# Idle products, an earlier root and earlier sums in the drain of a fused tower kernel, a second PSUM bank for two image pieces, and a last tile in halves

## The chip, the cores and the metric

One Trainium2 chip, one of its cores. The metric is the device time of one execution in microseconds (us), the median of several runs; lower is better.

## The reference

A batch of 64 images of 2 x 104 x 104 goes through three layers (fp32). `tok`: each image is stacked with its four shifts, normalised over all of it, scaled and shifted by maps, and cut into 8 x 8 patches by a convolution, which gives 169 tokens of 128. `attn`: attention with exponential features, 8 heads of 64. `ffn`: a mixture of 8 experts, 2 for each token.

```python
h = tok(x)                                         # [64, 169, 128]
n = layernorm(h)
q', k' = exp(q @ projT), exp(k @ projT)            # q, k, v from n @ WqkvT, by head
out = (q' @ (k'T @ v)) / (q' @ sum(k') + 1e-6)
h = h + out @ WoutT + bout
n = layernorm(h)
topv, topi = top_k(n @ Wg, 2); w = softmax(topv)
for e in experts:
    y += gw[..., e] * ((silu(n @ W[e]) * (n @ V[e])) @ W2[e])
h = h + y
```

## The kernel before, in words

**Tokens.** Two images (338 tokens) are a pair; there are 32 pairs, in 8 groups of 4. Each engine runs a program of its own, and semaphores order them. A loop of steps `n = 0 .. 34` is a software pipeline: in step `n` part `a` does the convolution and first layernorm of pair `n`, part `b` the projections and attention sums of pair `n - 1`, part `c` the normalisation, the attention output and the second layernorm of pair `n - 2`, part `d` the choice of experts of pair `n - 3`. `k = n % 4` is the step's place in its group `g`. Steps 32, 33 and 34 are the drain: `a` is missing in the first, `a` and `b` in the second, and only `d` is left in the third. In each of them other engines' chains have to end before TensorE can go on.

Within a group, the next group's images are turned into patch layout in seven pieces (`front_piece`): TensorE transposes a piece into PSUM bank 0 (L477), and VectorE multiplies it by gamma on the way out (L826). `TURN` gives the pieces to four places of steps k = 1, 2 and 3; `front(3)`, the last place of a step, has a piece for k = 1 and for k = 2. All pieces use bank 0, so `front(3)` waits until the piece of `front(2)` is read out. Bank 3 holds the turned tokens (L721), which VectorE has read when it sets `xT_low`.

VectorE's part of a step, in order: the reciprocals of the attention's sums (L905, L907, L919, L925), the convolution's output (L938), layernorm sums, `normalise` (L883), the choice of experts (`choose`, L1057 to L1073), the attention's result (L988), `place` (L1083 to L1100), a piece, the second layernorm (L832, L835), `best`, a piece. On TensorE `broadcast` (L559) waits for the reciprocals; `rank` (L579, L580) counts tokens per expert and waits for `choose`; `k_tokens` are L715 to L717, the attention output is L679.

**Routing.** POOL computes the inverse roots of the layernorms (`root`, L1315 and L1317) and sends each token's row to its expert's region with indirect DMAs (`scatter`, L1336), six for a pair. In step 33 (`d` and `c`, not `late`) it issues the DMAs of chunks 0 and 1 (four), then the root, then the two of chunk 2. The root feeds `choose` of step 34.

**Experts.** 92 tiles of 256 rows. For a tile TensorE turns the rows (L1442), does the hidden products in four blocks (`hidden`, L1457, banks 0 to 3), ScalarE the silu (L1532), VectorE the product (`product`, L1569), TensorE the down product into bank 4 or 5 (`down`, L1474, 16 instructions for two halves of 128 rows), VectorE scales the rows (`scale`, L1575 and L1577), and POOL adds them to the output with two indirect accumulating DMAs (`add`, L1631). An add waits until the adds of other tiles that could touch the same rows have landed; VectorE's `scale` waits for the adds that read its buffer. Tile 0 begins within the drain: its first two hidden blocks, the turn of tile 1 and the other two blocks are TensorE's `expert_tensor(pe, "first")` at the start of step 34; its four products are VectorE's, behind `place` of that step. Tile 1's `hidden` waits for tile 0's product of the same block. Between tiles 0 and 3 VectorE also computes the table of the other tiles.

`idle_products` (L573) are products whose result nobody reads; five of them stand in step 33 before the turn of tile 0.

## Time and profile before

| | us |
|---|---|
| median of 3 runs | 1150.2 (1149.58 to 1151.85) |
| profiled execution | 1150.7 |
| span of its core | 1148.9 |
| PE busy | 1089.3 (95%) |
| DVE busy | 881.0 (77%) |
| ACT busy | 561.7 (49%) |
| POOL busy | 614.4 (53%) |

The profiled execution's time is what a run's timer gives; its span runs from the first to the last instruction in the trace. PE is TensorE, DVE VectorE, ACT ScalarE, POOL GpSimd; a busy PE is one that has a matmul under way, at whatever clock. A granted clock of 1.00 is 2.4 GHz, 0.50 is 1.2 GHz. The tokens' loop runs to about 640 us, the drain to about 682 us, the experts from there on.

### The profile page before, as it was taken

To read this page: it belongs to the slowest core of one execution; us is meant where nothing else is said; L and a number is where in the kernel's file an instruction comes from. 1 tells how busy PE (TensorE), PEld (TensorE's weight loads), DVE (VectorE), ACT (ScalarE), POOL (GpSimd) and SP (SyncE) were. 2 spreads that over 40 slices of the span, in tenths; PEclk is the share of its full clock that TensorE was granted. 3 is DMA by queue.
4 is the path that set the end of the run, shared out by engine and by line. 5 is a ranking of instruction groups with operands and counts; after the bars stand their busy time and mean duration, and the time that the engine had idled before them with its cause. 6 is when DMAs were issued, how large, how long until landed. Compare 5 with 4: busy or idle time off the path is not lost.

```text
span 1148.9 us, 29991 instructions
## 1 busy us (share of the span) xinstructions
PE 1089.3 (95%) x8596; PEld 925.0 (81%) x8597; DVE 881.0 (77%) x3333; ACT 561.7 (49%) x1307; POOL 614.4 (53%) x656
## 2 busy tenths in 40 slices
PE   4999999999999999999999869899999999999995
PEld 3677777777777777777776569899999999999995
DVE  6568788887887878878867677677777777777774
ACT  3535435436355354363343425555555555555552
POOL 1103545444445454454444367576767676677675
PEclk9999999999999999999999889999999999999998
DMA  8270121310301312110110324344434443344343
GB/s 173 50 193 21 46 64 34 77 33 30 81 31 41 70 32 79 30 32 30 33 32 30 106 73 78 43 60 51 55 53 55 55 55 53 53 53 55 53 55 30
DMA packets 76011, 65.51 MB, mean 57 GB/s; under 512 B 12338, under 2 KB 66802, under 8 KB 75926
## 3 DMA queue, kind: packets, MB, share of 16 engines
q0 software_dynamic: 32704, 24.99, 15.6%
q1 hardware_dynamic: 43078, 39.16, 13.9%
q8 instruction: 42, 0.69, 0.3%
q10 hardware_dynamic: 144, 0.32, 0.1%
q14 instruction: 43, 0.35, 0.1%
HBM read 32.72 MB, written 31.71 MB: 56 GB/s over the span
## 4 chain that ended last, share of the span: by engine, by line
PE 77%; DVE 14%; issue 3%; DMA 2%; ACT 1%; SPq 1%; POOL 1%; POOLq 0%; DVEq 0%; ACTq 0%
PE bank L1457 21%; PE bank L1474 13%; PE bank L679 7%; PE bank L728 5%; PE bank L741 4%; PE bank L715 4%; PE bank L716 3%; PE bank L717 3%; PE bank L734 3%; DVE rparts L919 3%; DVE patches L826 2%; PE bank L477 2%; DVE rparts L925 2%; PE bank L607 2%; DVE rden L907 2%
## 5 line engine op out<-in xcount | busy, mean ns | idle before, releaser
L1631 POOL DMA_INDIRECT out_rows<-yo,dest x184 | 312.9, 1701 | 136.9 <-issue 102.0
L1457 PE MATMUL bank<-xT_e,wv 128*128 128x256 f32 x2208 | 289.5, 286 | 3.9 <-DVE hid L1569 3.0
L1457 PEld LDWEIGHTS bank<-xT_e,wv 128*128 128x128 f32 x2208 | 271.8, 189 | 4.4 <-issue 3.4
L1336 POOL DMA_INDIRECT sorted_rows<-xrow_all,sloti x192 | 191.2, 996 | 85.5 <-issue 54.2
L1532 ACT ACTIVATE sil<-bank 128x256 f32<-128x256 f32 x368 | 141.3, 385 | 170.4 <-PE bank L1457 159.8
L1474 PE MATMUL bank<-w,hid 128*128 x1472 | 181.3, 277 | 4.4 <-DVE hid L1569 4.3
L1474 PEld LDWEIGHTS bank<-w,hid 128*128 128x128 f32 x1472 | 173.0, 193 | 5.7 <-issue 5.7
L1551 DVE TENSOR_TENSOR wv<-wv_all,wv 128x1024 fp32r<-128x1024 f32 x92 | 113.5, 1233 | 65.9 <-PE bank L1457 58.6
L1569 DVE TENSOR_TENSOR hid<-sil,bank 128x256 f32<-128x256 f32 x368 | 143.8, 416 | 25.1 <-ACT sil L1532 21.2
L1243 ACT ACTIVATE attn<-bank 128x256 f32<-128x256 f32 x128 | 49.4, 386 | 159.6 <-PE bank L717 159.6
L1513 ACT CAST wv<-wv_all 128x1024 fp32r x92 | 96.2, 1046 | 30.0 <-issue 27.9
L1357 POOL COPY xrow_all<-xrow_all 128x384 f32<-128x384 f32 x32 | 16.9, 528 | 159.9 <-issue 149.3
L614 PE MATMUL bank<-patches,wct 128*128 128x338 f32 x320 | 99.5, 458 | 0.1
L826 DVE TENSOR_TENSOR patches<-bank,gam 128x416 f32<-128x416 f32 (+3 forms) x160 | 71.7, 502 | 22.5 <-PE bank L477 21.7
L679 PE MATMUL bank<-attn 128*128 128x169 f32 x512 | 81.4, 312 | 0.6 <-DVE attn L883 0.6
L614 PEld LDWEIGHTS bank<-patches,wct 128*128 128x128 f32 x320 | 58.2, 190 | 28.3 <-DVE patches L826 0.4
L741 PE MATMUL bank<-wvo,attn 128*64 128x136 f32 x1024 | 77.1, 290 | 2.3 <-ACT attn L1292 1.4
L679 PEld LDWEIGHTS bank<-attn 128*128 128x128 f32 x512 | 75.6, 192 | 2.3 <-DVE attn L883 0.8
L1258 ACT ACTIVATE attn<-bank 128x512 f32<-128x512 f32 x96 | 57.5, 599 | 33.9 <-PE bank L717 33.9
L1238 ACT COPY attn<-bank 128x272 f32<-128x272 f32 x128 | 50.0, 390 | 44.2 <-PE bank L741 41.3
L741 PEld LDWEIGHTS bank<-wvo,attn 128*64 128x64 f32 x1024 | 57.7, 138 | 14.7 <-ACT attn L1238 6.9
L728 PE MATMUL bank<-attn,xtok 128*128 128x512 f32 x128 | 68.3, 615 | 0.0
(213 smaller groups left out, 1806.4 us busy)
## 6 DMA issues: line engine op xcount, KB each, us to landing
xr<-sorted_rows SPq DMA_DIRECT2D x92, 130.0 KB
raw<-in_x SPq DMA_DIRECT2D x64, 84.5 KB
raw<-in_x SPq DMA_DIRECT2D x60, 78.0 KB
out_rows<-attn SPq DMA_DIRECT2D x64, 58.5 KB
sorted_rows<-xrow_all,sloti POOLq DMA_INDIRECT x192
out_rows<-yo,dest POOLq DMA_INDIRECT x184, 3.4
wv_all<-in_L_ffn_W SPq DMA_DIRECT2D x8, 256.0 KB, 5.0
wv_all<-in_L_ffn_V SPq DMA_DIRECT2D x8, 256.0 KB, 5.2
```

The source lines that it names most:

```text
L614: t = pe.matmul(bank[1][:, 0:PT], wct[:, q], patches[:, par, q, 2 * k:2 * k + 2].rearrange("p b t -> p (b t)"), start=(q == 0), stop=(q == 4))
L679: t = pe.matmul(bank[7][:, TOK * i:TOK * i + TOK], mm[:, pc, i, j, 0:D], qf[:, pc, j, TOK * i:TOK * i + TOK], start=(j == 0), stop=(j == 3))
L728: pe.matmul(bank[(6, 1)[i]][:, :], xtok[:, p, i], kf[:, i], start=True, stop=False)
L741: t = pe.matmul(o_[64 * (h % 2):64 * (h % 2) + 64, col:col + D + HEADS], gT[:, i, NF * h:NF * h + NF], wvo[:, h], start=True, stop=True)
L1336: po.indirect_dma_start(sorted_rows, bass.IndirectOffsetOnAxis(sloti[:, p, j, ch:ch + 1], 0), xrow[:, p, j, ch], None).then_inc(s(f"scatte ...
L1457: q = pe.matmul(bank[fc][:, TT * m:TT * m + TT], wv[:, w, w_, m, cols], xT[:, p, x_], start=(w_ + x_ == 0), stop=(w_ == 1))
L1474: q = pe.matmul(bank[4 + p][:, D * a:D * a + D], hid[:, p, fc, 128 * a:128 * a + 128], w2[:, bass.ds(e, 1), fc].rearrange("p e n -> p (e n ...
L1513: ac.copy(wv[:, w, 0].rearrange("p m n -> p (m n)"), wv_all[:, bass.ds(e, 1)].rearrange("p e m n -> p (e m n)")).then_inc(s("w_high"), 1)
L1532: ac.activation(sil[:, fc % 2], bank[fc][:, 0:TT], ACT.Silu).then_inc(s("silu_done"), 1)
L1551: ve.tensor_tensor(wv[:, w, 1].rearrange("p m n -> p (m n)"), wv_all[:, bass.ds(e, 1)].rearrange("p e m n -> p (e m n)"), wv[:, w, 0].rear ...
L1569: ve.tensor_tensor(hid[:, p, fc], sil[:, fc % 2], bank[fc][:, TT:2 * TT], ALU.mult).then_inc(s("h_done"), 1)
L1631: po.indirect_dma_start(out, bass.IndirectOffsetOnAxis(dest[:, p, a:a + 1], 0), yo[:, p, a], None, compute_op=ALU.add).then_inc(s(f"added{ ...
```

## The change

Six edits:

1. `front(3)` on TensorE waits for `xT_low` of the step and turns its piece into bank 3, without waiting for the piece before it (`ahead` = 1); VectorE reads it there.
2. Idle products: five more in step 32 before the broadcasts, nine in place of five in step 33, and in step 34, into bank 4, three before `rank` and four behind it. One product is two instructions of L573.
3. On POOL in step 33 one of the four DMAs ahead of the second root goes behind it.
4. VectorE does the first two products of tile 0 before `place` of step 34, no longer behind it.
5. The last tile's down product writes its second half to bank 4, behind a wait for the tile before; a semaphore tells of the first half, VectorE scales each half as it comes, and POOL adds the first half while the second is under way.
6. The last two tiles' adds on POOL are written out behind the loop.

```diff
                 def front(i):
                     if fr and k in TURN and TURN[k][i] is not None:
-                        front_piece(g + 1, TURN[k][i])
+                        if i == 3:
+                            pe.wait_ge(s("xT_low"), n + 1)
+                            front_piece(g + 1, TURN[k][i], 3, 1)
+                        else:
+                            front_piece(g + 1, TURN[k][i])
...
+                if n == NPAIR:
+                    idle_products(5)
                 if n == NPAIR + 1:
-                    idle_products(5)
+                    idle_products(9)
                     expert_tensor(pe, "turn")
                 if n == NPAIR + 2:
                     expert_tensor(pe, "first")
+                    idle_products(3, 4)
                 if d and not a and not b:
                     rank()
+                if n == NPAIR + 2:
+                    idle_products(4, 4)
...
-                        front_piece(g + 1, TURN[k][i], 1 - par)
+                        front_piece(g + 1, TURN[k][i], 1 - par, 3 if i == 3 else 0)
...
+                if n == NPAIR + 2:
+                    expert_vector(ve, "products")
                 if n > NPAIR:
                     place(md, pd, 96 * half(-3))
...
                 if d and not late:
                     wait_alone(po, setup_met, (s("sloti_ready"), md + 1), (s("w1_ready"), md + 1))
-                    scatter(range(2 if c else 1))
+                    scatter(range(1))
+                    if c:
+                        scatter(range(1, 2), which=(0,))
                 if c:
                     wait_alone(po, setup_met, (s("ln2_mv"), NCH * (mc + 1)), (s("ln2_x"), mc))
                     root(rstd[:, 1], mv[:, 1, :, 1], vare[:, 1], 1e-5, K("mhalf")[:, 0:NCH], s("ln2_vare"), s("ln2_rstd"), mc)
...
-                        scatter(range(1, 2), which=(1,))
+                    scatter(range(1, 2), which=(1,))
                     scatter(range(2, NCH))
...
+            last = isinstance(t, int) and t == NT - 1
+            if last:
+                pe.wait_ge(s("y_scaled"), NT - 1)
             for a in range(2):
+                if last and a == 1:
+                    q.then_inc(s("y_half"), 1)
                 for fc in range(4):
-                    q = pe.matmul(bank[4 + p][:, D * a:D * a + D], hid[:, p, fc, 128 * a:128 * a + 128],
+                    q = pe.matmul(bank[4 + (1 - p if last and a == 1 else p)][:, D * a:D * a + D], hid[:, p, fc, 128 * a:128 * a + 128],
...
-        scale(NT - 1, NT // 2 - 1, 1)
+        ve.wait_ge(s("y_half"), 1)
+        ve.wait_ge(s("meta_done"), NT)
+        ve.wait_ge(s("added1"), 32 * (NT // 2 - 1) + 16)
+        ve.tensor_copy(dest[:, 1], meta_[:, 1, :, 1])
+        ve.tensor_scalar(yo[:, 1, 0], bank[5][:, 0:D], meta_[:, 1, 0, 0:1], None, ALU.mult).then_inc(s("half_scaled"), 1)
+        ve.wait_ge(s("y_done"), NT)
+        ve.tensor_scalar(yo[:, 1, 1], bank[4][:, D:2 * D], meta_[:, 1, 1, 0:1], None, ALU.mult).then_inc(s("y_scaled"), 1)
...
+                scaled = (s("half_scaled"), 1) if last else (s("y_scaled"), t + 1)
+                wait_alone(po, met, scaled, (s(f"added{p}"), 32 * h + 16), (s(f"added{1 - p}"), others))
...
             for a in range(2):
+                if last and a == 1:
+                    po.wait_ge(s("y_scaled"), NT)
...
+        add(NT - 2, NT // 2 - 1, 0)
+        add(NT - 1, NT // 2 - 1, 1, True)
```

`expert_vector(ve, "products")` is `product(0, 0, 0)` and `product(0, 0, 1)`, which `step` of tile 0 now leaves out.

## Rows read from the trace of the kernel before

**Rows 1.** The page, the chain that ended last: shares by engine.

```profile
PE 77%; DVE 14%; issue 3%; DMA 2%; ACT 1%; SPq 1%; POOL 1%; POOLq 0%; DVEq 0%; ACTq 0%
```

**Rows 2.** Windows: each engine's busy time (instructions), granted clock, DMA share, GB/s.

```profile
643.40:650.20 6.80, 6.01 (x16) 4.26 (x15) 3.52 (x18) 2.30 (x5) 1.85 (x3) 0.50 1.13 302
667.30:670.70 3.40, 3.40 (x13) 3.40 (x13) 1.30 (x10) 0.10 (x1) 2.68 (x6) 0.50 0.36 97
680.90:687.80 6.90, 6.03 (x28) 6.06 (x29) 5.68 (x20) 1.85 (x5) 2.98 (x3) 0.51 0.38 107
```

**Rows 3.** Waits of PE, 30 to 640 us: total, times, longest.

```profile
PE bank L477 <- DVE patches L826: 5.3, 13, 0.5
```

**Rows 4.** Timeline, a k = 1 step: start us, us, instruction [idle before <- releaser].

```profile
211.68 0.55 PE L477 MATMUL bank<-cst,nrm 104*128 104x104 f32 x4 [0.33 <-DVE patches L826]
...
215.30 0.25 DVE L905 TENSOR_SCALAR dsum<-bank 128x86 f32<-128x86 f32 x1 [0.69 <-PE bank L607]
```

**Rows 5.** Timeline, the k = 2 step behind it.

```profile
233.45 1.17 DVE L826 TENSOR_TENSOR patches<-bank,gam 128x104 f32<-128x104 f32 x5
...
234.66 0.25 DVE L905 TENSOR_SCALAR dsum<-bank 128x86 f32<-128x86 f32 x1
```

**Rows 6.** Timeline of the drain's first step (n = 32).

```profile
642.53 0.42 PE L559 MATMUL bank<-rparts,pick_head 104*128 104x340 f32 x1 [2.52 <-DVE rparts L925]
...
645.78 0.65 PE L559 MATMUL bank<-rparts,pick_head 104*128 104x340 f32 x1 [0.79 <-DVE attn L883]
...
659.70 2.43 PE L573 MATMUL bank<-cst 128*128 128x256 f32 x10
```

**Rows 7.** Timeline of the drain's second step (n = 33).

```profile
664.26 0.58 PE L559 MATMUL bank<-rparts,pick_head 104*128 104x340 f32 x2 [1.78 <-DVE rparts L925]
...
667.07 4.24 PE L679 MATMUL bank<-attn 128*128 128x169 f32 x16 [0.60 <-DVE attn L883]
...
673.58 0.95 POOL L1336 DMA_INDIRECT sorted_rows<-xrow_all,sloti  x1 [0.30 <-issue]
...
674.40 0.31 DVE L835 BATCH_NORM_AGGREGATE mv<-bns 128x2 f32<-128x6 f32 x3
...
675.87 0.19 POOL L1315 TENSOR_SCALAR vare<-mv 128x3 f32<-128x3 f32 x1
```

**Rows 8.** Timeline of the third step (n = 34) and the first expert tiles.

```profile
677.56 1.28 ACT L1307 ACT_TABLE_LOAD   x1
...
678.42 0.28 PE L579 MATMUL bank<-before,whole_numbers 128*128 128x32 f32 x1 [1.82 <-DVE before L1073]
...
678.96 0.64 ACT L1532 ACTIVATE sil<-bank 128x256 f32<-128x256 f32 x2
679.50 0.16 DVE L1083 TENSOR_SCALAR esum<-egap 128x3 f32<-128x3 f32 x1
...
681.22 0.73 DVE L1569 TENSOR_TENSOR hid<-sil,bank 128x256 f32<-128x256 f32 x2
...
681.77 2.90 PE L1457 MATMUL bank<-xT_e,wv 128*128 128x256 f32 x12 [2.96 <-DVE hid L1569]
...
687.65 0.74 DVE L1569 TENSOR_TENSOR hid<-sil,bank 128x256 f32<-128x256 f32 x2
```

**Rows 9.** Timeline of the first tiles' adds on POOL.

```profile
711.35 1.55 POOL L1631 DMA_INDIRECT out_rows<-yo,dest  x1 [1.00 <-issue]
...
720.00 1.55 POOL L1631 DMA_INDIRECT out_rows<-yo,dest  x1 [4.33 <-DMA out_rows<-yo,dest]
```

**Rows 10.** Timeline of the last tile.

```profile
1136.36 2.05 PE L1474 MATMUL bank<-w,hid 128*128 x16 [1.01 <-DVE hid L1569]
1137.24 1.55 POOL L1631 DMA_INDIRECT out_rows<-yo,dest  x1 [0.30 <-issue]
...
1138.52 0.60 DVE L1577 TENSOR_SCALAR yo<-bank,meta_ 128x128 f32<-128x128 f32 x2
1139.87 1.55 POOL L1631 DMA_INDIRECT out_rows<-yo,dest  x1 [1.08 <-issue]
```

More of the change, by code:

```diff
@@ L568, in q_feature, with idle_products @@
                              lambda a_: xT[:, pb, a_, 0:QW]).then_inc(s("q_mm"), 1)
-                def idle_products(count):
+                def idle_products(count, at=0):
                     for _ in range(count):
-                        pe.matmul(bank[0][:, 0:256], ident, cst[:, 0:256], start=True, stop=True)
+                        pe.matmul(bank[at][:, 0:256], ident, cst[:, 0:256], start=True, stop=True)
                 def rank():
@@ L1589, in step @@
                 low_w(t + 1, (w + 1) % 4)
-            product(t, p, 0)
-            product(t, p, 1)
+            if not (isinstance(t, int) and t == 0):
+                product(t, p, 0)
+                product(t, p, 1)
             if isinstance(t, int) and t == FIRST_TILES - 2:
@@ L1611, in vector @@
             return
+        if what == "products":
+            product(0, 0, 0)
+            product(0, 0, 1)
+            return
         if what == "low_x":
@@ L1618, in vector, with add @@
         steps(step, what)(ve)
-        scale(NT - 1, NT // 2 - 1, 1)
+        ve.wait_ge(s("y_half"), 1)
[5 more added lines that the diff above has]
+        ve.tensor_scalar(yo[:, 1, 1], bank[4][:, D:2 * D], meta_[:, 1, 1, 0:1], None, ALU.mult).then_inc(s("y_scaled"), 1)
     def gpsimd(po, what):
-        def add(t, h, p):
+        def add(t, h, p, last=False):
             if not (isinstance(t, int) and t == 0):
                 others = po.value_load(table[0:1, bass.ds(t, 1), 2], min_val=16, max_val=16 + 32 * NT)
-                wait_alone(po, met, (s("y_scaled"), t + 1), (s(f"added{p}"), 32 * h + 16), (s(f"added{1 - p}"), others))
+                scaled = (s("half_scaled"), 1) if last else (s("y_scaled"), t + 1)
+                wait_alone(po, met, scaled, (s(f"added{p}"), 32 * h + 16), (s(f"added{1 - p}"), others))
             else:
```

2 lines of the change are left out of this document (1 added, 1 removed).

## The prediction

> **What bounds the kernel now.** I read the chain that ended last first: three quarters of it is PE [rows 1]. So time is won only where PE, or what PE waits for, comes sooner. The waits of PE in the tokens' loop are next. One group is left, L477 behind L826, 13 times, 5.3 us in all [rows 3]: the transposes of `front(3)` wait for bank 0. The timeline then shows what each wait is worth. In the k = 1 step PE waits 0.33 us, and behind it VectorE's L905 waits 0.69 us for PE [rows 4]: PE is the late one. That leaves 5.3 - 6 x 0.33 = 3.3 for the seven k = 2 steps, 0.48 each. But there L905 starts at 234.66 with no wait, as its own L826 x5 ended at 233.45 + 1.17 = 234.62 [rows 5]: VectorE is the late one.
>
> The drain is the third view. PE waits 2.52 and 0.79 us in step 32, 1.78 and 0.60 in step 33, 1.82 and 2.96 in step 34 [rows 6 to 8], and behind each pair of waits the granted clock is 0.50, the lower of the two levels (1.2 GHz): for 6.8, 3.4 and 6.9 us [rows 2]. In the stretch of step 33 it is L679 that takes 4.24 us [rows 7], and half of 3.4 of it is the clock's; in that of step 34 the first hidden blocks of tile 1 take 2.90 [rows 8].
>
> From tile 4 on, the adds hold everything for a while: POOL starts its first add 1.00 us idle, so it waits for the data, and tile 5's waits 4.33 us for tile 4's add to land [rows 9]. That chain of landings is only carried along. What reaches tile 4's first add sooner reaches the end sooner.
>
> **The sum, part by part.**
>
> Bank 3 (edit 1). For k = 1, six groups: 6 x 0.33 = 2.0, inside VectorE's 0.69 of wait. For k = 2 the wait goes but VectorE's own chain is as late, so nothing, but for the first such step, which has no part `d`; its share is 5.3 - 6 x 0.33 - 6 x 0.48 = 0.4. Sum **2.4**. The added wait for `xT_low` costs nothing: that is set before the attention output. Behind it on PE stand only the `context_out` products. If it were late they would be too, and ScalarE's copies after them. Bounds: 0 (something else is as late as bank 0) and 5.3 (all the waits).
>
> The Trainium skill ("TensorE: Matmul & The Clock Gate", section "HAM oscillation") reports for its thin-M matmul kernel that PSUM double-buffering gave no further gain. By that this term would be 0 and the sum 3.9; here the row shows PE waiting for the bank, so I keep 2.4.
>
> Idle products. Five take 2.43 us [rows 6], 0.46 each in the middle of a row of them. *Step 32*: five fill 2.3 of the 2.52 us wait, so they cost nothing. If they keep the clock at 2.4 GHz, the stretch from 645.78, where PE gets its next broadcast, to 650.2 at 1.2 GHz, in which PE is busy throughout, takes half: 2.2, less 0.2 for what doesn't scale, **2.0**. The broadcast at 645.78 itself waits for `normalise` and stays. Bounds: 0 (the clock falls nevertheless: 1.5 us of wait are left before 645.78, its 0.79 and the 0.7 by which the work ahead of it, from 643.4 on, ends sooner) and 2.2. *Step 33*: four more take 1.8, against a wait of 1.78 [rows 7]; the turn of tile 0 and `rank` stand behind them and come that much later, which `place` hides. L679 at full clock takes 2.5 instead of 4.24, and VectorE and PE come 1.7 sooner. But POOL doesn't: its row of scatters is its own, and only the root's place in it counts. So alone this is worth 0.2, counted in the next term. *Step 34*: three products (1.4) fit in the 1.82 us before `rank`; `rank` waits for `choose`. It comes at 678.42 - 1.3 (next term) and takes 0.4; four products (1.8) behind it end at about 679.3, and what tile 1 waits for is there at 679.0: 0.3 of cost that doesn't decide, as below.
>
> Root and first sums (edits 3, 4). Before, the root starts at 675.87, behind four scatters, though the moments are there at 674.40 + 0.31 = 674.71 [rows 7]. With three ahead it starts behind 673.58 + 0.95 = 674.53 [rows 7], at 674.60 if the moments are there, which the faster L679 gives (0.2 later without). 1.27 sooner; the DMA moved behind it is POOL's time in either place, and the later scatters end when they did. VectorE's chain `choose`, scaling, products, `place` follows the root: 1.3 sooner. The two products swap places with `place`, which began at 679.50: from 678.25 on, at 0.73 us [rows 8], they end at about 679.0, not at 681.95; `place` begins there and ends 0.6 sooner than before, and the products' 0.73 then isn't behind it, so the chain past both stays 1.3 sooner. Of the silus (0.64 for two, from 678.96 on) [rows 8] the first is ready at about 678.05, 0.2 before VectorE asks. PE's tile 1 so starts at 679.3 instead of 681.77, and at full clock takes half: PE is ahead by over 4 us. It doesn't keep that: VectorE's products of tile 1 at 687.65 stand behind `place` and the first part of the table, without a wait for PE [rows 8], and are only 1.3 sooner. So PE waits again, for 2.5 us before tile 2's blocks, and there I expect the clock to fall once more, over work of which 1.3 us is slack. I take **1.1** of 1.3. Bounds: 0 (a long low clock there) and 4.4 (all that PE gains). POOL's first adds are its own queue; before tile 4's it has 1.00 us idle [rows 9], and about 0.4 of that stays after tiles 0 to 3 catch up.
>
> Last tile (edits 5, 6). The first half's eight products end at 1136.36 + 1.0; scaling takes 0.3 behind the copy; POOL starts 0.75 after its data (1139.87 against 1138.52 + 0.60) [rows 10]: 1138.6. But POOL is in the add of the tile before until 1137.24 + 1.55 = 1138.79 [rows 10], and 0.30 lies between its adds where nothing is waited for (the idle of 1137.24): 1139.1, **0.8** sooner. The second half's data are there by then. Bounds 0.3 (POOL takes the 0.75 behind its own end) and 1.3.
>
> Sum: 2.4 + 2.0 + 1.1 + 0.8 = **6.3**. From the profiled execution's 1150.7 that is 1144.4; the median of the runs lies 0.5 lower: **1143.9**.
>
> The Trainium skill ("ScalarE: Activation LUTs", section "What ACT_TABLE_LOAD costs") gives 1.28 us for a table load and 1.38 more for a drain at every switch, 2.66. The load's row agrees with the first number; the silu at 678.96 leaves no room for the second, with `esum_silu` between. By the page VectorE would stand before `place` for 1.2 us; that is a rival.
>
> **The rivals.**
>
> *The clock falls nevertheless* (0.25). For: 1.5 us of wait remain in step 32, and 2.5 in tile 1. In step 32 waits of 2.52 and 0.79 with work between held it down for 6.8 us [rows 2, 6]. Against: after the five products of step 33 the clock stayed up over 1.78 us. Step 32 then gives 0.3 and edits 3 and 4 nothing: 2.4 + 0.3 + 0.8 = 3.5, 1146.7.
>
> *VectorE stands behind the silu* (0.08). `place`, the last scatters and the whole table are queued behind the two products. With 1.2 us of wait the 1.1 is gone: 5.2, 1145.0. Against: no drain in the row, and that 0.2 of reserve.
>
> *Bank 3 gives nothing* (0.07), by something as late as the bank, or since the piece ends up waiting as before: 3.9, 1146.3.
>
> *The k = 2 wait counts too* (0.07). VectorE's tie is exact in one row; if its chain is carried by PE elsewhere, 6 x 0.48 = 2.9 more: 1141.0.
>
> *Slower: the idle products are run at 1.2 GHz* (0.03). Sixteen more or moved products stand in front of `broadcast`, `rank` and tile 1. At half clock one takes 0.91: step 32 overruns its wait by 2.0, step 33 by 4.0 (nine, 8.2, against 2.43 + 1.78), step 34 by 2.9 (seven, 6.4, against 4.8 - 1.3). With the two drain terms gone: 2.4 + 0.8 - 8.9, 5.7 slower, 1155.9. It decides once the overruns exceed the 6.3. Against: the clock is 1.00 where each row of them begins.
>
> Forecast 0.50. The range leaves out the slower rival and the tails: **1141.0 to 1147.5**. A measurement of this kernel tells about 0.2% (2.3 us) from no change, so faster means under 1147.9: all but the slow rival and part of the clock's: faster 0.92, same 0.05, slower 0.03.
>
> **What would show it.** L477 with no wait for L826, L905's wait in k = 1 at 0.36, a k = 2 step as long as before. Granted clock 1.00 through steps 32 and 33, L679 of step 33 at 2.5. The second root behind three scatters. Products of tile 0 ahead of L1083 with no wait for ACT. A new PE wait of 2 us or more before tile 2. Tile 4's first add about 5.5 sooner, the last add 6.3. Wrong if tile 4's add comes as much sooner as PE gains, or if tile 5's wait grows by what was won.

## The result, and the profile after

| | before | after |
|---|---|---|
| median of 5 runs each | 1149.58 (1147.55 to 1151.85) | 1142.14 (1140.54 to 1143.80) |
| profiled execution | 1150.7 | 1143.8 |
| span of its core | 1148.9 | 1142.0 |
| mean granted clock | 0.986 | 0.995 |

The ratio is 0.9925, 95% interval 0.9904 to 0.9945: faster, by less than 1%. The medians are 7.4 us apart, where 6.3 were forecast; the time lies in the range given. The changed kernel was timed twice more beside experiments: 0.9935 (0.9912 to 0.9957) and 0.9922 (0.9901 to 0.9944).

A total says little about the steps. So I took the lead of the changed kernel, the difference of two start times in the two timelines, at every place that both traces have. It falls apart into these terms (worked out from the timelines; each line's term is the lead's change since the line above; "first reciprocal" is the sum that VectorE reads for it, L905 before and L916 after):

```text
place (before, after)                                      lead    term   forecast
first reciprocal, step 2 (62.11, 62.66)                   -0.55   -0.55    0
first reciprocal, step 3 (81.12, 81.16)                   -0.04   +0.51    0.4
the same, step 31 (619.83, 617.30)                        +2.53   +2.57    2.0
the same, step 32 (639.46, 635.64)                        +3.82   +1.29    0
attention's result, step 32 (653.21, 647.52)              +5.69   +1.87    2.0
second root, step 33 (675.87, 669.82)                     +6.05   +0.36    1.3 (1.27)
tile 4's first add (711.35, 706.70)                       +4.65   -1.40   -0.2
last add (1141.72, 1134.88)                               +6.84   +2.19    0.8
```

**The loop.** The page first: the chain's head, whose PE share was 77% [rows 1].

```profile
PE 79%; DVE 11%; issue 3%; DMA 3%; ACT 1%; SPq 1%; POOL 1%; DVEq 0%; POOLq 0%; another core or an unknown queue 0%; ACTq 0%
```

The waits of PE from 30 to 637 us (total, times, longest) have no L477 any more; 5.3 us in 13 waits stood there before [rows 3]. The second line is partly new: it was 0.4 us in 2 waits.

```profile
PE bank L564 <- DVE rparts L936: 2.2, 1, 2.2
PE bank L649 <- DVE h1T L949: 1.5, 8, 0.2
PE bank L752 <- ACT attn L1305: 1.4, 1, 1.4
```

The timeline of the k = 1 step and the k = 2 step behind it, in the changed kernel:

```profile
210.94 0.58 PE L477 MATMUL bank<-cst,nrm 104*128 104x104 f32 x4
...
214.59 0.25 DVE L916 TENSOR_SCALAR dsum<-bank 128x86 f32<-128x86 f32 x1 [0.31 <-PE bank L613]
...
232.57 0.80 PE L613 MATMUL bank<-attn 128*32 128x86 f32 x32
...
232.74 1.17 DVE L837 TENSOR_TENSOR patches<-bank,gam 128x104 f32<-128x104 f32 x5
233.84 0.24 DVE L916 TENSOR_SCALAR dsum<-bank 128x86 f32<-128x86 f32 x1
```

L916's wait in k = 1 is 0.31, forecast 0.36, before 0.69 [rows 4]. From a k = 1 step to the next the lead grows by 0.35, as forecast, in each of six groups. From a k = 2 step to the next it grows by 0.11 each time, forecast 0. The row of PE that the reading of [rows 5] left out shows why. In the kernel before it is:

```profile
233.80 0.80 PE L607 MATMUL bank<-attn 128*32 128x86 f32 x32
```

It ends at 234.60, VectorE's own instruction at 234.62, and L905 starts at 234.66: the two engines were late together. In the changed kernel PE's row ends at 233.37, and L916 starts at 233.84, 0.07 before VectorE's instruction ahead of it ends (233.91). So PE comes half a microsecond sooner there, and VectorE passes on only 0.1 of it. PE now waits for VectorE instead: 0.2 us at L649, once behind each such step.

**Steps 32 and 33.** The timeline:

```profile
636.02 2.32 PE L579 MATMUL bank<-cst 128*128 128x256 f32 x10
638.71 0.42 PE L564 MATMUL bank<-rparts,pick_head 104*128 104x340 f32 x1 [0.36 <-DVE rparts L936]
...
641.97 0.42 PE L564 MATMUL bank<-rparts,pick_head 104*128 104x340 f32 x1 [1.48 <-DVE attn L894]
...
645.03 2.46 PE L690 MATMUL bank<-attn 128*128 128x169 f32 x16
...
654.01 4.15 PE L579 MATMUL bank<-cst 128*128 128x256 f32 x18
...
661.39 2.56 PE L690 MATMUL bank<-attn 128*128 128x169 f32 x16 [0.60 <-DVE attn L894]
```

and the windows (columns as in [rows 2]):

```profile
641.97:647.52 5.55, 5.55 (x29) 4.56 (x30) 2.60 (x4) 3.28 (x5) 2.24 (x3) 1.00 1.17 311
658.57:664.00 5.43, 3.98 (x20) 2.97 (x20) 4.22 (x20) 2.47 (x4) 3.15 (x5) 1.00 0.11 37
```

The five products fill 2.3 of the first wait, which was 2.52 [rows 6]; 0.36 of it is left. The second wait, for `normalise`, grows from 0.79 to 1.48. Still the granted clock is 1.00 behind the two, where it was 0.50 [rows 2]. The step gives 1.87. In step 33 the clock stays up as well, and the attention output L690 takes 2.56, where it took 4.24 [rows 7].

**The second root.** Timeline of POOL and VectorE in step 33:

```profile
665.13 1.23 DVE L1572 TENSOR_TENSOR wv<-wv_all,wv 128x1024 fp32r<-128x1024 f32 x1 [0.44 <-issue]
665.43 1.79 POOL L1349 DMA_INDIRECT sorted_rows<-xrow_all,sloti  x1 [0.56 <-issue]
667.04 0.31 DVE L846 BATCH_NORM_AGGREGATE mv<-bns 128x2 f32<-128x6 f32 x3
...
667.53 0.96 POOL L1349 DMA_INDIRECT sorted_rows<-xrow_all,sloti  x1 [0.30 <-DVE mv L846]
668.79 0.96 POOL L1349 DMA_INDIRECT sorted_rows<-xrow_all,sloti  x1 [0.30 <-issue]
...
669.82 0.19 POOL L1328 TENSOR_SCALAR vare<-mv 128x3 f32<-128x3 f32 x1
...
671.09 0.16 DVE L899 TENSOR_TENSOR gaps<-gap,rstd 128x3 f32<-128x3 f32 x1 [2.31 <-POOL rstd L1330]
```

The root is behind three scatters, as forecast, but the first takes 1.79 where all took 0.95 to 1.0 [rows 7]: it starts while VectorE subtracts a weight of 128x1024 (L1572). The moments (mean and variance, which the root needs) are there at 667.35, and the root waits 2.5 us for POOL.

**Step 34 and the first tiles.**

```profile
673.45 0.74 DVE L1590 TENSOR_TENSOR hid<-sil,bank 128x256 f32<-128x256 f32 x2
674.12 0.67 DVE L1096 TENSOR_SCALAR esum<-egap 128x3 f32<-128x3 f32 x1
674.23 1.79 PE L1472 MATMUL bank<-xT_e,wv 128*128 128x256 f32 x12
...
682.92 1.86 PE L1472 MATMUL bank<-xT_e,wv 128*128 128x256 f32 x12 [2.19 <-DVE xT_e L1583]
...
688.64 0.42 DVE L1583 TENSOR_TENSOR xT_e<-bank,xT_e 128x256 fp32r<-128x256 f32 x1
...
689.81 0.17 DVE L1596 CAST dest<-meta_ 128x2 uint32<-128x2 f32 x1 [0.75 <-remote]
...
693.52 0.49 DVE L1604 CAST table<-bank 1x261 int32<-1x261 f32 x1
694.97 1.84 SPq L1441 DMA_DIRECT2D xr<-sorted_rows  x2
...
697.45 0.44 PE L1457 MATMUL bank<-cst,xr 128*128 128x128 f32 x2 [0.73 <-DMA xr<-sorted_rows]
```

The two products stand ahead of `place` with no wait for ACT. PE's wait before `rank` is 1.84, as long as before (1.82), though three idle products fill part of it now: PE comes sooner, and the root hardly does. Tile 1's blocks take 1.79 in place of 2.90 [rows 8]. PE then waits 2.19 ahead of tile 2's blocks, forecast 2.5, and the clock falls behind it (0.50 from 684.5 to 687.6). The products, the blocks and the wait before tile 2 are as forecast. Not forecast are a wait of 0.75 ahead of L1596, for which the profile names no instruction, and PE's wait of 0.73 for tile 5's rows.

**Adds and last tile.** POOL in the first tiles, and the last tile:

```profile
706.70 1.55 POOL L1666 DMA_INDIRECT out_rows<-yo,dest  x1 [1.00 <-issue]
708.56 2.47 POOL L1666 DMA_INDIRECT out_rows<-yo,dest  x1 [0.30 <-issue]
713.58 2.10 POOL L1666 DMA_INDIRECT out_rows<-yo,dest  x1 [2.55 <-DMA out_rows<-yo,dest]
...
1130.29 2.05 PE L1495 MATMUL bank<-w,hid 128*128 x16 [1.02 <-DVE hid L1590]
1131.16 1.55 POOL L1666 DMA_INDIRECT out_rows<-yo,dest  x1 [0.30 <-issue]
1131.56 0.35 DVE L1649 TENSOR_SCALAR yo<-bank,meta_ 128x128 f32<-128x128 f32 x1
...
1133.02 1.55 POOL L1666 DMA_INDIRECT out_rows<-yo,dest  x1 [0.30 <-issue]
1134.88 1.55 POOL L1666 DMA_INDIRECT out_rows<-yo,dest  x1 [0.30 <-issue]
```

The last tile's first add starts 0.30 behind the add before it, not 1.08 [rows 10]: 0.78, as forecast. Tile 5's first add waits 2.55 for a landing, where it waited 4.33 [rows 9].

### The profile page after: what moved, and what is told of

It is laid out like the page before. It is cut to its first block, busy times and chain, and to the rows that moved or that the text cites. A ratio compares the mean times of both kernels' runs of the same rounds, so it can differ in the third digit from the quotient of the medians.

```text
span 1142.0 us, 30063 instructions
## 1 busy us (share of the span) xinstructions
PE 1089.6 (95%) x8628; PEld 924.8 (81%) x8629; DVE 882.1 (77%) x3333; ACT 561.5 (49%) x1307; POOL 614.4 (54%) x656
## 4 chain that ended last, share of the span: by engine, by line
PE 79%; DVE 11%; issue 3%; DMA 3%; ACT 1%; SPq 1%; POOL 1%; DVEq 0%; POOLq 0%; another core or an unknown queue 0%; ACTq 0%
PE bank L1472 20%; PE bank L1495 13%; PE bank L690 7%; PE bank L739 5%; PE bank L752 5%; PE bank L620 4%; PE bank L726 4%; PE bank L728 3%; PE bank L727 3%; PE bank L745 3%; PE bank L477 2%; PE bank L708 2%; DVE rparts L930 2%; PE bank L613 2%; DMA out_rows<-yo,dest 2%
## 5 line engine op out<-in xcount | busy, mean ns | idle before, releaser
L1572 DVE TENSOR_TENSOR wv<-wv_all,wv 128x1024 fp32r<-128x1024 f32 x92 | 113.3, 1232 | 65.4 <-PE bank L1472 51.2
L690 PE MATMUL bank<-attn 128*128 128x169 f32 x512 | 79.9, 308 | 0.6 <-DVE attn L894 0.6
L690 PEld LDWEIGHTS bank<-attn 128*128 128x128 f32 x512 | 73.9, 189 | 2.0 <-DVE attn L894 0.8
```

Of the source, the lines that this page charges most:

```text
L690: t = pe.matmul(bank[7][:, TOK * i:TOK * i + TOK], mm[:, pc, i, j, 0:D], qf[:, pc, j, TOK * i:TOK * i + TOK], start=(j == 0), stop=(j == 3))
L1572: ve.tensor_tensor(wv[:, w, 1].rearrange("p m n -> p (m n)"), wv_all[:, bass.ds(e, 1)].rearrange("p e m n -> p (e m n)"), wv[:, w, 0].rear ...
```

## The experiments

After this reading there were two theories. By the one, the forecast's terms are right as they stand, and the surplus over 6.3 us and the loss before tile 4's add are chance. By the other, some terms are larger or smaller than their working, and the drain has a bound that the forecast lacked. Each experiment was timed in five rounds against the kernel before on its own chip, so ratios are compared, not times. The stages of all traces stand in one table behind the first four.

**One part alone.** Edit 1 alone on the kernel before:

```diff
-                        front_piece(g + 1, TURN[k][i])
+                        if i == 3:
+                            pe.wait_ge(s("xT_low"), n + 1)
+                            front_piece(g + 1, TURN[k][i], 3, 1)
+                        else:
+                            front_piece(g + 1, TURN[k][i])
...
-                        front_piece(g + 1, TURN[k][i], 1 - par)
+                        front_piece(g + 1, TURN[k][i], 1 - par, 3 if i == 3 else 0)
```

> The kernel before with edit 1 alone (front(3) in bank 3). Theory (only the k = 1 waits and the first k = 2 wait count): 2.5 us faster, and VectorE's L905 of the last token step (n = 31) 2.5 sooner; the waits of L477 for L826 are gone. Rival (every wait of L477 counts): 5.3 us faster. Rival (something else is as late as bank 0): no difference. The wait of 2.2 us in step 31, behind the early table, is not touched; whether the granted clock falls behind it, as before, may differ from run to run, and is worth 1.3 us.

Measured: 0.9970 (0.9959 to 0.9981), 3.4 us, from 12 runs. The waits of L477 for L826 are gone. The lead of its reciprocal grows from -1.10 in step 2 to +2.16 in step 31: 3.26, in the same parts as in the changed kernel. So the term is 3.1 to 3.3, not 2.4, and neither 0 nor 5.3.

The changed kernel without the new idle products (five in step 33 stay):

```diff
-                if n == NPAIR:
+                if n == NPAIR + 1:
                     idle_products(5)
-                if n == NPAIR + 1:
-                    idle_products(9)
...
-                    idle_products(3, 4)
...
-                if n == NPAIR + 2:
-                    idle_products(4, 4)
```

> The changed kernel with the idle products of the kernel before (five in step 33, none in steps 32 and 34). Theory (they hold the clock up, and that pays in step 32): 1.9 to 2.3 us slower than the changed kernel, 5.2 faster than the kernel before; granted clock 0.50 again behind the waits of steps 32, 33 and 34, the attention output of step 33 at 4.2 us. Rival (they only fill waits and the clock would have stayed up by phase): no difference from the changed kernel.

Measured: 0.9954 (0.9937 to 0.9971). Against 0.9922 to 0.9935 for the whole change the idle products are worth 2 to 4 us, with an uncertainty of as much. In its trace the clock falls in steps 32 and 33 again. In step 34 it doesn't, though that was expected: PE's waits there are 0.81 and 1.25, and tile 1's blocks take 1.68 without an idle product.

Edits 3 and 4 alone on the kernel before:

```diff
-                    scatter(range(2 if c else 1))
+                    scatter(range(1))
+                    if c:
+                        scatter(range(1, 2), which=(0,))
...
+                if n == NPAIR + 2:
+                    expert_vector(ve, "products")
...
```

> The kernel before with edits 3 and 4 alone (one scatter behind the root of step 33, tile 0's first two products ahead of place). Theory: root of step 33 behind three scatters, 1.0 us sooner, and tile 4's first add 0.8 to 1.0 sooner: 0.9 us faster. Rival (VectorE's copy of weights runs over the POOL's scatters and lengthens one by 0.8, as in the changed kernel): the root 0.3 sooner and the time 0.2 faster. Rival (the landing of tile 4's add sets the end): no difference.

Measured: 0.9997 (0.9984 to 1.0010). The root is 1.0 sooner behind the attention's result, as forecast, and of that nothing can be timed.

Edits 5 and 6 alone (of the diff only the calls are shown):

```diff
...
-        scale(NT - 1, NT // 2 - 1, 1)
+        ve.wait_ge(s("y_half"), 1)
...
+        add(NT - 2, NT // 2 - 1, 0)
+        add(NT - 1, NT // 2 - 1, 1, True)
```

> The kernel before with edits 5 and 6 alone (last tile in halves). Theory: POOL's own queue bounds the first half; its last two adds 0.77 us sooner, the time 0.8 faster, which may be within the measurement; the trace shows 0.30 between the last four adds. Rival (POOL takes its 0.75 behind the end of the add before): 0.3 sooner.

Measured: 0.9999 (0.9983 to 1.0015). The trace shows the 0.78 at the last add; the time doesn't, and an interval of nearly 2 us to each side can't. This execution also kept its clock at 2.4 GHz through step 32, without any idle product there (a window, columns as in [rows 2]):

```profile
640.00:650.00 10.00, 6.00 (x29) 4.27 (x28) 7.00 (x30) 3.81 (x9) 4.29 (x5) 1.00 0.84 225
```

So the fall that edit 2 prevents doesn't come in every execution. The attention's result of step 32 came 1.87 sooner by that, and the root of step 33 only 0.86, because the subtraction of the weight and a scatter met here as well, in a kernel whose drain is that of the kernel before:

```profile
670.63 1.23 DVE L1557 TENSOR_TENSOR wv<-wv_all,wv 128x1024 fp32r<-128x1024 f32 x1 [0.43 <-issue]
670.75 1.94 POOL L1336 DMA_INDIRECT sorted_rows<-xrow_all,sloti  x1 [0.30 <-issue]
```

**The stages.** Worked out from the timelines, in us: from the first reciprocal of step 31 to that of 32, on to the attention's result of 32, to the root of 33, to tile 4's first add, to the last add. The last column is the sum of the third and fourth. Each row is one execution, so a difference of a few tenths between two rows is no finding.

```text
kernel                     31-32  32-result  root   tile 4   last    3rd+4th
before                     19.63  13.75      22.66  35.48    430.37  58.14
e1 bank 3 alone            19.60  13.74      22.66  36.21    428.94  58.87
e3 root and sums           18.35  14.11      21.65  36.08    428.84  57.73
e4 tail alone              18.35  11.88      23.67  35.31    428.12  58.98
e2 no new idle products    18.33  13.80      21.65  36.21    428.26  57.86
after                      18.34  11.88      22.30  36.88    428.18  59.18
after, second trace        19.61  11.89      22.44  37.73    428.45  60.17
after, third trace         19.86  11.89      21.66  37.07    427.93  58.73
e5 products in step 31     18.33  11.88      22.42  36.96    427.96  59.38
e6 products before tile 2  18.33  11.88      22.44  37.10    428.52  59.54
e8 weights sooner          18.33  11.90      22.47  37.64    427.67  60.11
e10 destination sooner     18.33  11.89      21.43  39.51    427.97  60.94
e11 root behind two        19.85  11.88      21.66  38.19    428.26  59.85
e12 no idle in step 34     18.33  11.89      22.42  40.04    427.81  62.46
e13 three of them          18.33  11.90      21.59  37.71    427.98  59.30
e14 pads sooner            18.35  11.88      22.41  38.87    427.11  61.28
e15 pads and destination   18.34  11.89      22.30  37.42    427.85  59.72
e16 these and the root     18.34  11.89      21.16  36.99    427.89  58.15
```

Three things are to be seen. The first column has 18.3 in some rows and 19.6 to 19.9 in others, with and without the change and both within the changed kernel: it differs from one execution to the next. The second is 11.9 wherever the five products stand (13 traces), 13.7 to 14.1 in four of the five without them. And the last column, the drain from the attention's result to tile 4's add, is 57.7 to 59.0 without the new idle products and 58.2 to 62.5 with them: a stage that gives nothing back, whatever was made faster in it. From the first reciprocal of step 32 to tile 4's add it was 71.9 us before and is 71.1, 72.1 and 70.6 in the changed kernel: 0.6 less on average, where 3.1 were forecast (2.0 and 1.1). e4 shows that this isn't all the edits' doing: its fast step 32 gained 1.87, and 1.03 of that reached tile 4's add (70.9). In e2, without the new idle products, it is 71.7, so of what they are worth in the timings (2 to 4 us) the traces show 0.4 here. The next experiments ask for each.

**Step 31.** A wait of 2.2 us for the reciprocals, like that of step 32, stands there.

> The changed kernel once more, beside its own variants. 7 us faster than the kernel before (0.9925 to 0.995). If the phase theory holds, the stretch behind the wait of step 31 is at 1.2 GHz in some executions and at 2.4 GHz in others, and runs differ by 1 to 3 us.

Measured: 0.9935 (0.9912 to 0.9957); in this trace the clock fell in step 31, which took 19.61.

```diff
+                if n == NPAIR - 1:
+                    idle_products(4)
```

> The changed kernel with four idle products more in step 31, ahead of the broadcast that waits 2.2 us for the reciprocals behind the early table. Theory (whether the clock falls behind that wait is chance, worth 1.3 us where it does): the granted clock is 1.00 through step 31 in the trace, the median up to 0.7 us below the changed kernel's, and the spread of the runs narrower. Rival (the clock stays up there without them): no difference.

Measured: 0.9937 (0.9917 to 0.9958); 18.33, as in both other traces with these products (e13, e16), while 5 of the other 15 have 19.6 to 19.9. Its six runs lie within 1.1 us, those of the changed kernel beside it within 5.6. The median isn't lower: 1143.71 against 1143.80. Three traces can't show that the products hold the clock, as 10 of the other 15 kept it too.

**Ahead of tile 2.** Eight small products fill PE's wait of 2.2 us there:

```diff
+            if isinstance(t, int) and t == 2:
+                pe.wait_ge(s("rank_read"), NPAIR)
+                for _ in range(8):
+                    pe.matmul(bank[5][:, 0:128], ident, ident, start=True, stop=True)
```

> The changed kernel with eight idle products of 128 columns ahead of tile 2's first hidden block, in the 2.2 us that PE waits there (new in the changed kernel). Theory (the fall of the clock behind that wait costs little, as VectorE is later than PE): the down product of tile 1 takes 1.95 instead of 3.2 us, and the time is at most 0.4 faster. Rival (it costs what I took off the term, or more): 1 us faster.

Measured: 0.9923 (0.9900 to 0.9945). PE's clock stays up from 684 to 688, and tile 4's add isn't sooner (59.54). That fits the forecast that PE's speed there is slack; but in this trace the clock fell at 673 us, ahead of tile 1's blocks.

**The subtraction beside the scatter.** `low_w(1)` (L1572) ahead of the attention's result, so that it isn't under way when the first scatter begins:

```diff
-                if n == NPAIR + 1:
-                    expert_vector(ve, "weights", range(1, 2))
...
                 if n == NPAIR + 1:
                     expert_vector(ve, "rows", 0)
+                    expert_vector(ve, "weights", range(1, 2))
```

> The changed kernel with VectorE's low half of tile 1's weights (L1572, 1.2 us) moved ahead of the attention's result of step 33, out of the POOL's scatters. Theory (a 128 x 1024 subtraction on VectorE holds up a POOL instruction that is under way; the first of the three scatters took 1.79 us under it, and 0.96 otherwise): that scatter takes 1.0 and the root starts 0.8 sooner, though the attention's result is 0.7 later; the time 0.5 to 0.8 faster. Rival (the scatter's 1.79 has another cause): the root no sooner, and the time the same or up to 0.7 slower.

Measured: 0.9938 (0.9916 to 0.9960). The scatters take 1.0 again, but POOL's copy of 128x384 ahead of them overlaps the subtraction now and takes 1.56, not 0.51, so that they start 0.96 later: the root is where it was (22.47). So the scatter is as fast as elsewhere once the subtraction isn't beside it, the copy pays in its place, and nothing is gained.

**The unnamed wait, the root's place, the products of step 34.** All three on the changed kernel.

```diff
...
+            if isinstance(t, int) and t == 0:
+                ve.wait_ge(s("meta_done"), 2)
+                ve.tensor_copy(dest[:, 1], meta_[:, 1, :, 1])
             product(t, p, 2)
```

> The changed kernel, but the destination of tile 1's rows (L1596, SBUF to SBUF) is cast right behind the copy of its meta data in tile 0's part, no longer in scale(1). What is asked is what the 0.75 us are that the profile leaves unnamed ahead of L1596 in tile 1. Theory A: in each kernel that has this wait the cast starts within 0.1 us of the end of an indirect add's instruction on POOL (after: POOL 688.14 + 1.58 = 689.72, cast 689.81), while the scaling behind it reads PSUM. So VectorE's cast is held by POOL's DMA_INDIRECT. Then the scaling L1598 of tile 1 now starts within 0.2 us of the end of xT_e (L1583), the wait of 0.5 to 1.2 us is gone, and the table's cast L1604 stands 0.4 to 1.0 us closer to xT_e of tile 2 than in the changed kernel (4.88 us), unless that cast is then held itself. The time: 0 to 0.8 us below the changed kernel's. Rival B: the wait is for something that scale(1) itself has to have (the down product's semaphore, or its code): then L1598 waits the same 0.5 to 1.2 us and nothing moves.

Measured: 0.9933 (0.9920 to 0.9945). Its trace:

```profile
686.23 1.23 DVE L1572 TENSOR_TENSOR wv<-wv_all,wv 128x1024 fp32r<-128x1024 f32 x1 [0.55 <-issue]
686.35 2.60 POOL L1670 DMA_INDIRECT out_rows<-yo,dest  x1 [0.30 <-issue]
...
688.04 0.42 DVE L1583 TENSOR_TENSOR xT_e<-bank,xT_e 128x256 fp32r<-128x256 f32 x1
688.53 0.61 DVE L1599 TENSOR_SCALAR yo<-bank,meta_ 128x128 f32<-128x128 f32 x2
...
692.01 0.49 DVE L1605 CAST table<-bank 1x261 int32<-1x261 f32 x1
...
695.36 8.24 SPq L1441 DMA_DIRECT2D xr<-sorted_rows  x3
...
697.63 0.44 PE L1457 MATMUL bank<-cst,xr 128*128 128x128 f32 x2 [1.80 <-DMA xr<-sorted_rows]
698.57 3.48 PE L1495 MATMUL bank<-w,hid 128*128 x16 [0.50 <-issue]
```

The wait is gone, and the table stands 3.97 behind xT_e, not 4.88, as theory A had it. But its reason isn't shown: in e13 the same cast was moved and the scaling itself waited 1.21. That e10 had none may be because its first add was stretched to 2.60. The table's 0.9 brought nothing, since tile 5's rows weren't issued sooner. What SP's queue waited for says why (waiting line, releaser, total, times, longest):

```profile
SPq L1441 <- DMA sorted_rows<-cst: 1.9, 1, 1.9
SPq L447 <- DVE table L1605: 1.5, 1, 1.5
```

Past the table it waited 1.9 for the pad writes to land (L373: eight writes of 130 KB that fill the ends of the experts' regions). PE waited 1.80 for the rows, and behind that wait its clock fell: the down product took 3.48, not 2.05, and VectorE's next scaling 2.83 of wait. That is the 39.51.

```diff
                     scatter(range(1))
-                    if c:
-                        scatter(range(1, 2), which=(0,))
...
```

> The changed kernel, with two in place of three indirect DMAs ahead of the second root in step 33. Theory A: in the changed kernel the root's place was spoilt by the first of the three (1.79 us beside VectorE's subtraction of 128x1024, 0.96 without it), so it starts at 669.82 although the moments stand at 667.35. Behind two it starts at once behind the moments, about 667.6, VectorE takes rstd when it has found the best experts, 668.8 in place of 671.1: 2.2 us sooner, and the stretch from the attention's result of step 33 to ... the root shrinks by about 2.2. Of this 0.5 to 2 us reach tile 4's first add (the scatters behind the root are POOL's and end when they did; the rows of tiles 3 to 5 need them). Time 0.5 to 2.0 below the changed kernel. Rival B: the rows of the last tiles bound tile 4's add, as tile 5's rows do in PE's waits: the root comes sooner and the add within 0.3 of where it was, no change in time.

Measured: 0.9923 (0.9910 to 0.9936). The DMA taken out here goes behind the root. The root came 21.66 behind the attention's result, 0.64 sooner and not 2.2: in this execution the clock fell in step 33 (L690 4.24), so the moments were late (667.92, the root at 668.08). Tile 4's add didn't come sooner (59.85). This run doesn't tell the theories apart. e16 below has the same edit with the clock up: the root came 21.16 behind, 1.1 sooner than in the changed kernel, behind a first scatter of 2.00.

Without the seven products of step 34:

> The changed kernel without the seven idle products of step 34. Theory A (they are worth little, since VectorE and POOL set the end there): tile 1's first hidden blocks take 2.9 in place of 1.79 us at the lower clock, tile 2's wait before its blocks is shorter by 1 to 2 us, and the stretch from tile 1's root to tile 4's first add (36.9 to 37.7 in the changed kernel) stays or shrinks by up to 0.7. Time within 1 us of the changed kernel, either way. Rival B, the forecast's own: the clock there is worth 1.1 with the sooner root: 1 us slower, the stretch 1 us longer.

Measured: 0.9937 (0.9921 to 0.9952), the same as with them. Tile 1's blocks took 2.90 at the lower clock, as expected; PE's wait before tile 2 was 2.45, not shorter than 2.19. The stretch grew to 40.04, by more than the rival's 1 us. In its last part tile 5's rows came late (PE waited 1.62) and the clock fell behind that wait, as in e10; whether the missing products have a part in it, one trace doesn't tell.

> The changed kernel with the sooner destination of tile 1, the root behind two scatters, four idle products (eight instructions) in step 31 and eight small ones ahead of tile 2. Sum of what each theory gives: 0.6 for the destination (0 by the rival), 1.2 for the root (0 by the rival), 0.6 for step 31, where the clock fell in some executions and not in others and cost 1.3 us when it did, 0 to 0.3 ahead of tile 2: 2.4 below the changed kernel by theory A, 0.6 to 0.9 by the rivals. If the rows of tile 5 bound the adds, PE's wait for them grows by what is won.

Measured: 0.9935 (0.9912 to 0.9958), six runs from 1136.79 to 1145.96. The sum of the supposed gains gave none that can be timed.

**The pad writes.** All eight in one go, ahead of tile 4's rows (e14); with the sooner destination (e15); with the root behind two scatters and the products in step 31 as well (e16):

```diff
-            pad_ends(sp, range(0, E // 2))
+            pad_ends(sp, range(0, E))
             expert_sync(sp, "early_rows", 4)
-            pad_ends(sp, range(E // 2, E))
```

> The changed kernel with all eight pad writes (L373) issued in one go, ahead of the rows of tile 4 in SP's queue, in place of four before and four behind. Theory A: the pad writes bound tile 5's rows only where the table stands before they land. In the changed kernel SP waits 2.7 us for the table, so the rows are still issued at the table plus 1.4 us; nothing but PE's wait for their landing gets shorter (from 0.4 to 1.6 down to under 0.7), as there is less traffic beside them. Tile 4's rows come 2 us later, at about 687 to 689, and PE turns them at 691: covered. Time within 1 us of the changed kernel beside it. Rival B, the pad writes are the whole bound: 1 to 2 us faster.

> The same with the sooner destination of tile 1. Theory A: now table and pad writes are both ahead: the rows of tile 5 are issued 1.4 us behind the table with no wait for the pad writes (1.9 us with the destination alone), PE's wait for them is under 0.7 us in place of 1.8, its clock stays up between 697 and 704, and the stretch from the second root of step 33 to tile 4's first add is 36.0 to 36.9 in place of 39.5. Time 0.5 to 2 us below the changed kernel beside it. Rival B: something else holds tile 5's rows or tile 4's add, and the stretch stays over 37.

> The same, with the second root behind two scatters and four idle products in step 31 as well. Theory A: 0.7 to 1 us sooner at the root and up to 1.3 in step 31 on top: 1.5 to 3 us below the changed kernel beside it, the stretch from the root to tile 4's add 36.5 to 37.5 (the root is sooner, POOL's scatters aren't). Rival B: the gain stays in the stretch as before, and the time is within 1 us of the changed kernel.

> The changed kernel once more, for comparison on the same chip: 0.9925 to 0.9940 of the kernel before, the stretch from the second root to tile 4's first add 36.9 to 37.7 us.

Measured, in this order: 0.9939 (0.9920 to 0.9957), 0.9933 (0.9914 to 0.9953), 0.9927 (0.9907 to 0.9948), and the changed kernel beside them 0.9922 (0.9901 to 0.9944). PE's wait for tile 5's rows is gone in all three, and SP's wait for the pad writes too: they were what held those rows in e10. So e14's rival, by which the pad writes are the whole bound, is out. The wait moved by one tile:

```profile
676.90 11.95 SPq L373 DMA_DIRECT2D sorted_rows<-cst  x8
689.33 12.15 SPq L1440 DMA_DIRECT2D xr<-sorted_rows  x4
691.84 0.44 PE L1456 MATMUL bank<-cst,xr 128*128 128x128 f32 x2 [1.46 <-DMA xr<-sorted_rows]
```

(e15.) Tile 4's rows are issued at 689.33 (in e14 at 691.80), where 687 to 689 were expected, and PE waits 1.46 for them (1.67 in e14, 1.08 in e16). With destination and pads the stretch from the root is 37.42 in place of 39.51 (36.0 to 36.9 expected), with the root as well 36.99; the changed kernel's own is 36.9 to 37.7. e16 has the shortest way from step 32's reciprocal to tile 4's add of all traces, 70.0, but its runs are no faster than the changed kernel's. No version was clearly faster than the changed kernel: e6 came nearest to it (0.9923 where the changed kernel beside it had 0.9935), and here the best ratio is the changed kernel's own.

## Why the prediction was right, and where not

**Bank 3 (2.4 forecast, 3.1 to 3.3 measured).** Mechanism right: PE is late in k = 1, VectorE in k = 2. The size was off by 0.7 to 0.9 in three places: 0.11 in place of 0 in each of six k = 2 steps, 0.5 in place of 0.4 in the first one, and 0.35 in place of 0.33 in k = 1. The sentence that mis-sized it reads "VectorE's own chain is as late, so nothing". It rests on VectorE's row alone; PE's ended 0.02 before it, so 0.1 of each wait of 0.48 counted. The rival that k = 2 counts in full gave 2.9 more and is out. So is the rival that bank 3 gives nothing. The Trainium skill ("TensorE: Matmul & The Clock Gate", "HAM oscillation") reports no further gain from PSUM double-buffering for its thin-M kernel. This case differs: the row had shown a wait for the bank, and a second bank gave 3 us.

**Step 32 (2.0 forecast, 1.87 measured).** Right for the step: with waits of 0.36 and 1.48 left, the clock stayed at 2.4 GHz in all 13 traces with the five products. What the forecast lacked is that without them it doesn't always fall (e4 had 11.88), and that not all of it is passed on: of e4's 1.87 only 1.03 reached tile 4's add. The rival that it falls nevertheless is out for this step.

**Root and first sums (1.1 forecast; 0.3 to 1.1 without the new idle products; with them the stage from the attention's result to tile 4's add is longer than before by 0.6 to 2.0, 1.2 on average over three traces).** This is the step that failed: a gain of 1.1 was forecast, and a loss of 1.2 came. In the changed kernel's first trace the root gave 0.36 in place of 1.27, and the way from the root to tile 4's add cost 1.40 in place of 0.2. The root's order alone works as computed: 1.0 sooner in e2 and e3, where L679 is slow. The forecast then let the faster L679 add 0.2 ("which the faster L679 gives"). In fact VectorE's subtraction, which comes sooner by it, falls onto POOL's first scatter, which takes 0.8 to 1.1 longer; the root is at 22.3 to 22.5, not 21.4. With 0.83 us added the 0.36 is 1.19, near the forecast's 1.27. Step 32 does the same: in e4, with L679 slow, the subtraction fell onto the second scatter. In the four traces of this kind in which the two don't overlap (e10; the third of the changed kernel, e11 and e13, in which the clock fell in step 33 and made VectorE late again) it is at 21.4 to 21.7. That much is shown. For the way from the root to tile 4's add the cause is not shown. What's left there meets two queues that the forecast hadn't looked at: VectorE's unnamed wait of 0.5 to 1.4 in tile 1's scaling, and tile 5's rows, behind the table and SP's pad writes. The forecast counted POOL's and VectorE's queues in the first tiles, and not SP's. But taking those waits away one by one (e10, e14) moved them to another place and made nothing faster, so what bounds this stage stays open. The silu rival is out: products with no wait for ACT, the load 1.28 (671.51 to 672.79) and the next ACTIVATE at 672.80, so nothing of a drain behind it.

**Last tile (0.8 forecast, 0.78 measured).** Right in each row.

**Slower (0.03).** Each row of idle products ran at a granted clock of 1.00 in the changed kernel's profile.

**The sum.** 6.84 of lead at the last add against 6.3 looks closer than it is. In it are +1.29 from step 31 and about +1.4 from the stretch behind tile 4's add, where before's profile has 430.37 and the three kernels with one edit 428.8 to 428.9 (with 0.8 added to e4 for its last tile). Most of that lies in one wait: tile 5's first add starts 8.65 behind tile 4's in before and 6.97 in e1, which has the same drain. Both are chance of that one profile, which the forecast was made against; the -0.55 at the start is too. What the edits did in the traces is about 3.1 + 1.9 - 1.2 + 0.8 = 4.6. The runs say 7.4, 7.8 and 9.3 in three timings (ratios of 0.9922 to 0.9935). So that the total came near 6.3 is luck in part: a term that was lost is made up for by something that no term has. The intervals are wide (about 2 us and more to each side), and the way from the start to step 2's reciprocal alone is 60.0 to 64.2 us over the traces, so chance may be in it; but where the other 3 to 5 us would be, no single trace of a kernel can tell, and it stays open.

## What to carry to other kernels

Before a term counts as won, ask what runs at the new time. A faster engine can lay one of its instructions onto another engine's and slow that one, here by 0.8 to 1.1 us. Look at all queues up to the point where the work joins, SP's too. When an instruction starts with no wait, look at both engines that it could have waited for: a tie hides the second. If the clock falls behind a wait of TensorE, the wait costs more than its length; here filling it gave 1.87 us in one step. The fall comes in some executions only, so read several traces before putting a number on it. A stage that takes back each gain made in it has another bound than the one worked on.

## What the runs showed of the hardware

**POOL's indirect DMAs and VectorE's subtraction.** An indirect DMA that starts while VectorE subtracts a 128x1024 weight takes longer by about what is left of the subtraction, less 0.1 (the scatters took 0.96 otherwise, the adds 1.62):

```text
kernel  subtraction           POOL instruction starts   left of it   longer by
after   665.13 to 666.36      665.43 (scatter, 1.79)    0.93         0.83
e12     663.61 to 664.83      663.70 (scatter, 2.01)    1.13         1.05
e10     686.23 to 687.46      686.35 (add, 2.60)        1.11         0.98
e11     685.47 to 686.69      686.26 (add, 1.92)        0.43         0.30
```

Where the scatter began first (e10: 665.29 against 665.52) it took 0.99. The subtraction took 1.22 or 1.23 each time: beside these DMAs POOL alone pays. Beside POOL's copy of 128x384 both paid in before's trace: the copy took 1.30 (0.51 otherwise) and the subtraction 1.43. The Trainium skill ("GPSIMD Engine Reference", "1. Specifications") says that POOL shares its SBUF interfaces with VectorE and contends with VectorE's instructions that have two SBUF inputs; these rows agree, since both inputs of this subtraction lie in SBUF.

**An unnamed wait.** In 12 of the 13 traces of the changed kernel and its variants with idle products in step 32 VectorE waits 0.5 to 1.4 us in tile 1's scaling for nothing that the profile names, in none of the other five. In all but e11 it ends within 0.1 us of the end of an indirect add on POOL (after: 688.14 + 1.58 = 689.72, the cast at 689.81). That looks as if POOL held VectorE; but in e12 the same cast of tile 2 starts at 693.59, within an add that runs from 692.47 to 694.02, without a wait (in the changed kernel at 694.38, within 693.11 to 694.66), and e13 moved the cast away and had the wait. Its cause is open.

**The clock.** It fell to 1.2 GHz behind waits of 2.2 us in step 31 in some executions (before, e1, e11 and two of the three of the changed kernel) and not in others with the same instructions. In step 33, with nine idle products in the wait and only 0.80 and 0.60 of it left, it still fell in e11, e13 and the third trace of the changed kernel. In step 34 it fell behind PE's wait of 1.8 before `rank` in e5, e6, e14 and the second trace of the changed kernel, and not in the first, whose wait was 1.84.
